# The first sum of squares of every node tile from a centred product with features on partitions

## What is computed

```python
def _layernorm(x, axis=-1, eps=1e-05):
    m = jnp.mean(x, axis=axis, keepdims=True)
    v = jnp.var(x, axis=axis, keepdims=True)
    return (x - m) / jnp.sqrt(v + eps)

x = _layernorm(x + _L0_gnn_ref(x, L0_gnn_proj_cosim, L0_gnn_W_ffn, L0_gnn_b_ffn, src, dst), axis=-1)
x = _layernorm(x + _L1_gnn_ref(x, edge_attr_2, src, dst, ...), axis=-1)
x = _layernorm(x + _L2_gnn_ref(x, edge_index, ...), axis=-1)
x = _layernorm(x + _L3_gnn_ref(x, edge_index, ...), axis=-1)
```

## Time and profile before

| | us |
|---|---|
| median of 3 runs | 2573.97 |
| lowest, highest | 2572.82, 2577.59 |
| the profiled execution | 2577.51 |
| its span, first to last instruction | 2575.7 |
| first node stretch (block of lines 1182 to 1305) | about 886 to 1213 |
| second node stretch (block of lines 1462 to 1525) | about 1438 to 1715 |
| mean granted clock of TensorE | 0.748 |

### The profile page before, as it was taken

One profiled execution on the slowest core, in us unless ns is written; L12 is line 12 of the kernel. 1 busy time (PEld: TensorE's weight loads), 2 busy tenths in 40 slices (PEclk: granted clock), 3 DMA queues, 4 the chain that ended last, 5 costly groups with the idle time before them and its releaser, 6 DMA issues. The chain is left out here.

```text
span 2575.7 us, 25825 instructions
## 1 busy us (share of the span) xinstructions
PE 1392.9 (54%) x5738; PEld 832.2 (32%) x5738; DVE 1867.6 (73%) x3900; ACT 791.9 (31%) x1636; POOL 1423.4 (55%) x1382
## 2 busy tenths in 40 slices
PE   1433444444666588887466577634888543333231
PEld 1332333331333354443233455421333221212120
DVE  3877777875767589998688699977888675455542
ACT  1222222222545355554122355531222110101010
POOL 6777777735777576662000577730000277777776
PEclk9656555555877699999688899976888666566666
DMA  5433333431111233332011244420000011101010
GB/s 176 119 110 108 110 104 98 119 91 33 52 44 49 58 102 106 108 105 74 20 39 39 87 128 127 127 78 16 31 27 27 28 23 23 25 23 24 22 22 13
DMA packets 120400, 174.79 MB, mean 68 GB/s; under 512 B 36128, under 2 KB 42382, under 8 KB 120340
## 3 DMA queue, kind: packets, MB, share of 16 engines
q1 hardware_dynamic: 74836, 129.98, 15.0%
q0 software_dynamic: 43904, 43.81, 8.6%
q10 hardware_dynamic: 1600, 0.33, 0.1%
HBM read 88.48 MB, written 86.74 MB: 68 GB/s over the span
## 5 line engine op out<-in xcount | busy, mean ns | idle before, releaser
L461 POOL DMA_INDIRECT GA<-table,look_i x588 | 608.0, 1034 | 493.5 <-PEq L1473 213.0
L467 PE MATMUL P<-ident,GA 128*128 128x128 f32 x500 | 105.3, 348 | 411.6 <-DMA GB<-in_x,dst_i 198.9
L491 PE MATMUL P<-center,work 128*128 128x128 f32 x800 | 152.1, 352 | 210.9 <-DVE work L1697 174.2
L266 POOL DMA_INDIRECT GA<-in_x,src_i x196 | 210.6, 1074 | 83.5 <-issue 70.8
L1637 POOL DMA_INDIRECT out_x<-work,seg_i x196 | 205.0, 1046 | 59.8 <-issue 59.5
L1629 POOL DMA_INDIRECT GA<-table,look_i x196 | 200.2, 1022 | 59.8 <-issue 59.4
L266 POOL DMA_INDIRECT GB<-in_x,dst_i x196 | 196.9, 1004 | 59.7 <-issue 59.7
L509 ACT ACTIVATE work<-P 128x512 f32<-128x512 f32 x100 | 59.7, 597 | 518.6 <-PE P L491 518.1
L491 PEld LDWEIGHTS P<-center,work 128*128 128x128 f32 x800 | 135.9, 257 | 242.2 <-issue 113.1
L467 PEld LDWEIGHTS P<-ident,GA 128*128 128x128 f32 x500 | 71.1, 176 | 441.7 <-issue 222.3
L610 PE MATMUL P<-center,work 128*128 128x128 f32 x984 | 160.6, 313 | 91.1 <-ACT work L653 67.4
(11 more groups left out here) (332 smaller groups left out, 3448.9 us busy)
## 6 DMA issues: line engine op xcount, KB each, us to landing
table<-work SPq DMA_DIRECT2D x175, 256.0 KB, 2.4
XN<-in_x SPq DMA_DIRECT2D x98, 256.0 KB, 2.7
out_x<-work SPq DMA_DIRECT2D x98, 256.0 KB, 2.4
GA<-table,look_i POOLq DMA_INDIRECT x784, 2.4
XN<-in_src_pad SPq DMA_DIRECT2D x13, 512.0 KB
cols<-in_dst_pad SPq DMA_DIRECT2D x50, 128.5 KB, 4.7
table<-XN SPq DMA_DIRECT2D x1, 6400.0 KB
src_wide<-in_src_pad SPq DMA_DIRECT2D x12, 512.0 KB, 5.4
```

Source lines behind the costliest of these rows:

```text
L266: pool.indirect_dma_start(buf[:, s % 2, j * D:(j + 1) * D], None, a["x"], bass.IndirectOffsetOnAxis(ap=look[:, s * 8 + j:s * 8 + j + 1], a ...
L461: pool.indirect_dma_start(GA[:, par, j * D:(j + 1) * D], None, table_k, bass.IndirectOffsetOnAxis(ap=look[:, s * 8 + j:s * 8 + j + 1], axis=0)
L467: ins = pe.transpose(dst[:, q * 128:(q + 1) * 128], src[:, q * 128:(q + 1) * 128], ident[:, :])
L491: ins = pe.matmul(norm_bank(par, far)[:, q * 128:(q + 1) * 128], W[par][4][:, q * 128:(q + 1) * 128], center[:, :], start=True, stop=True)
```

## The change

For each of the 98 node tiles: the centring product is formed with `center` as the fixed weight and all 512 columns of VT as the moving operand, so its result stands in `BN[par][1]` with features on partitions, 128x512. ACT squares it as before (line 616, now 622). The sum over features is now a sum over partitions, and PE forms it: `row_sums` takes each 128 columns of the squares as the weight and two columns of `total` as the moving operand, and puts two columns for each of the four pieces back into the first eight columns of `BN[par][1]`. ACT's root reads them there. DVE's first reduction falls away. The chained products stay as they were. The stage of each step stays too: the row sums are a new PE stage `node_pe2` in the slot of the root (d = 3), at yield 0. `dense_pe` and `dense_sum` stay in use in the edge block of lines 866 to 1041.

```diff
+        def row_sums(pe, dst, squares):
+            for q in range(4):
+                ins = pe.matmul(dst[:, 2 * q:2 * q + 2], squares[:, q * 128:(q + 1) * 128], total[:, 0:128:64], start=True, stop=True)
+            return ins
...
         def node_pe1(pe, T, n, par, k):
-            yield from dense_pe(pe, T, par, k, 0)
+            VT = W[par][0]
+            yield 0
+            pe.wait_ge(T("vt"), k)
+            if not (isinstance(k, int) and k == 1):
+                pe.wait_ge(T("y0"), k - 1)
+            pe.matmul(BN[par][1], center[:, :], VT, start=True, stop=True).then_inc(T("dense_mm"), 1)
+            for q in range(4):
+                ins = pe.matmul(BN[par][2][:, q * 128:(q + 1) * 128], VT[:, q * 128:(q + 1) * 128], chain[:, :], start=True, stop=True)
+            ins.then_inc(T("dense_mm"), 1)
+
+        def node_pe2(pe, T, n, par, k):
+            yield 0
+            pe.wait_ge(T("sq1"), k)
+            row_sums(pe, BN[par][1], W[par][1]).then_inc(T("ss1"), 1)
...
         def node_act2(act, T, n, par, k):
             yield 1
             act.wait_ge(T("ss1"), k)
-            double_root(act, T, par, 2, 0, "sd1")
+            act.activation(sm(par, 2), BN[par][1][:, 0:8], ACT.Sqrt, scale=(1.0 + EPS) / D, bias=eps_2).then_inc(T("sd1"), 1)
...
         def node_dve2(dve, T, n, par, k):
-            yield from dense_sum(dve, T, par, k, 0)
             yield 2
             dve.wait_ge(T("sd1"), k)
...
-            paced(pe, S, only(base, None, partial(node_pe0, pe), partial(node_pe1, pe)), owns, unrolled)
+            paced(pe, S, only(base, None, partial(node_pe0, pe), partial(node_pe1, pe), partial(node_pe2, pe)), owns, unrolled)
```

## The result

The changed kernel is slower: 2606.73 us, median of four runs (2605.72 to 2610.02), where before stands at 2575.43 (four runs, one more than in the table above; 2572.82 to 2577.59). The ratio is 1.012, with a 95% interval of 1.0102 to 1.0137. The direction was forecast, the size was not: +31 us, not +8, and the time lies outside the range. The profiled execution has a span of 2608.3 us.

A forecast was written before the change was run, and what follows sets the result against it. PE was taken to become the first stretch's bound, with POOL alone pacing the second: +8.5, 0 and -0.7 make about +8 us, 2582 beside the median of 2573.97, range 2570 to 2590.

The forecast's parts named there:

- First stretch, +8.5 us: Node stretch at 886 to 1213 us: 18 double slots +5.8, three +2.4, two at the edges +1.3, last slots -1.0.
- 12.84 us forecast: PE's need per first-stretch double slot (two node tiles, one edge super) after the change, against 12.52 us before.
- 0.88 us a tile: Price of the row sums on PE: eight loads of 128 weight columns at 0.11 us each.
- DVE and ACT were put at 11.5: What DVE and ACT would need per first-stretch double slot after the change, about 11.5 us.
- Second stretch, 0 us: Node stretch at 1438 to 1715 us: no change in time, since scans and copies remain beside POOL's gathers.
- POOL sets this pace alone: Second stretch: POOL's gathers follow back to back with only 0.30 us of issue between, so POOL bounds it.
- +3 to -12 us: Second stretch's possible move: -12 if all gather stretching vanished, +3 if the first ten double slots took the later pace.
- Row sums hidden in the second stretch: PE's row sums there fit in its 2.26 us wait for ACT per double slot, under POOL's pace: 0 us.
- DVE's saving is useless there, 0 us: Second stretch: removing DVE's reduction of 0.60 us a tile gains nothing, as POOL sets the pace.
- POOL gains: Rival: lighter DVE stretches fewer gathers; second stretch gains 6 to 12 us, first loses 8.5; 2573 us in all; chance 0.12.
- The direction, slower: Whole kernel: above 2579 us counted as slower, chance 0.60; same 0.29, faster 0.11.
- The tail, -0.7 us: After the last gather, DVE's last reduction falls away before the last scans and logits: -0.7 us.

The follow-up runs named there:

- half_sums: The change in the first stretch alone, with two row-sum products of four columns for four of two (half the rows unsummed): 2567.5 us, 0.9944 of before.
- bf16_first: The change in the first stretch alone, with squares written as bf16 and row sums formed with bf16 ones: 0.9949 of before.
- new_dummy: The changed kernel with the removed reduction put back on DVE as dead work in the second stretch only: 1.0047 of before.
- moved_psum: The changed kernel with the second stretch's scans run later, behind the first root's reciprocal, one operand read from PSUM (values meaningless): 1.0470 of before.
- after_split: The changed kernel with each scan of the second stretch cut into two of 256 columns: 1.0046 of before.

## Why the prediction was wrong

- **First stretch, +8.5 us: right in mechanism and price, small by 4.5.** 12.84 us forecast, 12.83 measured; 0.88 us a tile, 0.89 measured; half_sums confirms that loads are the price and PE the bound. That it met to 0.01 is in part luck: the same reckoning had 12.1 and 12.2 to 12.4 for one tile of two, and 12.38 and 12.59 came, and bf16_first, its row sums nearly free, took 11.73 where DVE and ACT were put at 11.5. By starts of scans, the 18 double slots gave 5.6 us (forecast 5.8) and the last three 2.1 (2.4). What was mis-sized is the rest: the double slots ahead of these gave 2.8 (forecast 1.3), and from the last double slot to the start of the second stretch it was 2.4 more, where I had 1.0 less.
- **Second stretch, 0 us: the step that failed.** The sentences were "I take 0, as scans and copies remain", and "POOL sets this pace alone". It measured +23.8 us. The scans and copies did remain, but what they cost depends on the moment at which a gather meets them, and that moment is set by DVE's work. I had the mechanism in hand: the earlier trace rows show the gather of 1.31 us beside the copy of line 568, and I sized its range by what before showed of it, +3 to -12 us. The upper bound had to come from the worst meeting: a gather that begins just inside a scan waits for 1.28 of scan and 0.15 of copy and pays up to 0.96 us, the next pays 0.35 at the second scan, and bias adds cost up to 0.5 each. The changed kernel comes near that: 1.65 us of excess in a double slot against 0.57, and over the stretch POOL's gathers took 24.2 us more (225.15 against 200.92). My range for this term ended at +3.
- **"A second stretch that moved by more than 3 us would refute that POOL's pace is its own."** It did; new_dummy shows that DVE's work moved it, and moved_psum that two SBUF operands are what shuts POOL out.
- **Row sums hidden in the second stretch: right.** PE's new work did not lengthen it: new_dummy has all of it at 10.73.
- **DVE's saving is useless there, 0 us: wrong.** Taking the reduction away cost some 19 us by phase, as new_dummy got them back. The rival "POOL gains" had the right place and the opposite sign.
- **The direction, slower, was right, but for 13 of the 31 us only;** the larger part came from a step put at nothing.
- **The tail, -0.7 us:** not visible beside the 4 us by which the rest of this execution differed.

## What to carry to other kernels

Where POOL issues indirect DMAs back to back, ask of every DVE instruction with two SBUF operands where in POOL's round it falls, and bound the cost of any change to DVE, a lighter DVE too, by the worst meeting and not by the one that the trace happens to show. An operand in PSUM takes the dependence of that instruction away (no run here shows time gained by it), and cutting such instructions limits it where DVE has room: after_split had 0.59 us of excess in place of 1.65. And an idle time is room for new work only if that work's operand is there when the idle begins.

## What the runs showed of the hardware

- A gather's indirect DMA on POOL takes 0.955 us. If it begins 0.12 to 1.1 us into a DVE scan of 1.28 us with two SBUF operands, it ends 0.58 us behind the copy that follows: begun at 0.12 it took 1.91, at 0.15 1.90, at 0.26 1.79, at 0.50 1.54, at 0.74 1.31, at 0.96 1.09. Begun 0.05 us ahead of the scan, or up to 0.07 into it, 0.95 to 0.96. Under a scan with one operand in PSUM it took 0.95 or 0.96, all 24 times.
- POOL did not get in between a scan and its copy, 0.03 to 0.04 us apart; it did between two scan pieces 0.15 us apart.
- Loading 128 columns of f32 weights costs 0.11 us a pass even if two columns follow; in bf16, 0.04 and one pass in place of two.
